# A two-layer graph-attention kernel: the next group's first products moved ahead of the last product, x2 made on VectorE, and three output tiles started from x2 in PSUM

## The reference, cut to what matters

```python
h = jnp.maximum(_layernorm(x), 0.0)
x = x + L0(h, adj)      # 12 heads of 32
h = jnp.maximum(_layernorm(x), 0.0)
x = x + L1(h, adj)      # 6 heads of 64

# L0
v = einsum('bnd,ade->bane', h, W); th = tanh(v)
attn = leaky(th @ w_src + (th @ w_dst)^T); attn = where(~adj, -999, attn); attn = softmax(attn)
feat = elu(attn @ v + b); gate = sigmoid(h @ H_w.T + H_b)
return gate * feat + (1 - gate) * h
# L1
q, k, v = h @ Wq + bq, h @ Wk + bk, h @ Wv + bv
return softmax(q @ k^T / 8 + mask) @ v @ Wf + bf
```

## Time and profile before

| | |
|---|---|
| median of 3 runs | 1011.37 us (1010.96 to 1014.32) |
| the profiled execution | 1006.25 us |
| its span | 1004.5 us |
| granted PE clock, mean of the span | 0.979 |
| PE busy | 926.7 us (92%) |
| PE weight loads busy | 817.8 us (81%) |
| DVE busy | 786.5 us (78%) |
| ACT busy | 641.2 us (64%) |
| POOL busy | 278.5 us (28%) |

### The profile page before, as it was taken

How to read it: one execution, slowest core, us unless ns; L and a number is a source line. 1 busy time by engine, 2 the same in 40 slices (tenths; PEclk the granted TensorE clock), 3 DMA queues, 4 the chain that set the end, 5 groups by cost and what they waited for, 6 DMA issues and landing times.

```text
span 1004.5 us, 24765 instructions
## 1 busy us (share of the span) xinstructions
PE 926.7 (92%) x9851; PEld 817.8 (81%) x9851; DVE 786.5 (78%) x1473; ACT 641.2 (64%) x1309; POOL 278.5 (28%) x337
## 2 busy tenths in 40 slices
PE   6599999999999999999999999999999999999595
PEld 5386888988888898888889888888988888898475
DVE  5877777879777787977778797777879777886804
ACT  5647658484865858486585848658584865857242
POOL 2224050331506033150603315060331506032210
PEclk9799999999999999999999999999999999999887
DMA  8303252231526223152522415252241525221102
GB/s 221 66 3 32 34 97 34 71 42 18 97 33 97 33 69 44 19 96 34 97 33 68 45 20 96 33 97 33 69 45 18 96 34 97 33 59 19 20 32 64
DMA packets 185077, 56.41 MB, mean 56 GB/s; under 512 B 166402, under 2 KB 184964, under 8 KB 184964
## 3 DMA queue, kind: packets, MB, share of 16 engines
q1 hardware_dynamic: 184964, 54.83, 31.2%
HBM read 17.07 MB, written 12.58 MB: 30 GB/s over the span
## 4 chain that ended last, share of the span: by engine, by line
PE 71%; DVE 22%; issue 2%; ACT 1%; SPq 1%; DMA 1%; POOL 0%; ACTq 0%; DVEq 0%; POOLq 0%
PE ps L694 12%; PE ps L696 12%; PE ps L695 12%; PE ps L761 8%; PE ps L765 7%; PE ps L762 7%; PE ps L680 5%; DVE p L1072 4%; DVE mx L1070 3%; DVE p L1044 3%; DVE x L1032 3%; PE ps L774 3%; DVE rs L1040 3%; PE ps L897 3%; PE ps L840 1%
## 5 line engine op out<-in xcount | busy, mean ns | idle before, releaser
L439 POOL TENSOR_TENSOR x_in<-x_in,ee 128x384 f32<-128x384 f32 x64 | 68.5, 1070 | 563.9 <-DVE ee L1057 563.9
L426 POOL TENSOR_TENSOR x_in<-x_in,bf_row 128x384 f32<-128x384 f32 x64 | 84.0, 1342 | 50.6 <-ACT p L459 50.6
L1070 DVE TENSOR_REDUCE mx<-ps 128x6 f32<-128x384 f32 x64 | 35.2, 550 | 75.8 <-PE ps L840 75.8
L1085 DVE COPY_PREDICATED_SCALAR z<-not_adj,masked 128x768 f32 x64 | 69.9, 1092 | 29.4 <-ACT z L550 29.4
L955 DVE TENSOR_TENSOR hT1l<-ps,hT1h 128x384 fp32r<-128x384 f32 x128 | 62.5, 549 | 26.0 <-ACT hT1h L464 26.0
L680 PE MATMUL ps<-ident,p 128*128 128x128 f32 x384 | 54.6, 287 | 26.9 <-DVE p L1044 15.5
L680 PEld LDWEIGHTS ps<-ident,p 128*128 128x128 f32 x384 | 44.6, 146 | 32.6 <-issue 18.3
L513 ACT ACTIVATE ps<-hb_all 128x384 f32<-128x384 f32 x56 | 27.6, 493 | 66.9 <-DVE x_in L1097 66.9
L531 ACT ACTIVATE QT<-ps,bq_col 128x512 f32<-128x512 f32 x48 | 33.0, 688 | 58.4 <-PE ps L765 58.4
L694 PE MATMUL ps<-Wf_hi,hT1h 128*128 128x384 f32 x192 | 67.6, 352 | 1.2 <-DVE x L1032 0.6
L432 POOL TENSOR_TENSOR x_in<-x_in,h 128x384 f32<-128x384 f32 x64 | 64.2, 1035 | 14.4 <-DVE Wf_lo L985 14.4
(11 more groups left out here) (134 smaller groups left out, 2815.7 us busy)
## 6 DMA issues: line engine op xcount, KB each, us to landing
x_in<-in_x_dram SPq DMA_DIRECT2D x16, 768.0 KB, 5.0
V<-v_tok SPq DMA_DIRECT2D x64, 192.0 KB, 5.8
V<-v_tok SPq DMA_DIRECT2D x128, 96.0 KB, 2.4
out_dram<-x_in SPq DMA_DIRECT2D x16, 768.0 KB, 3.5
x<-in_L_gnn_H_w_dram SPq DMA_DIRECT2D x1, 576.0 KB, 6.1
QT<-in_L_gnn_W_dram SPq DMA_DIRECT2D x3, 192.0 KB, 6.9
thT<-in_L_gnn_Wq_dram SPq DMA_DIRECT2D x1, 576.0 KB, 5.5
z<-in_L_gnn_Wk_dram SPq DMA_DIRECT2D x1, 576.0 KB, 6.5
```

What stands on the lines that cost most here:

```text
L426: pool.tensor_tensor(x_in[:, j % 3, t], x_in[:, j % 3, t], bf_row[:], ALU.add).then_inc(x2_biased, 1)
L439: pool.tensor_tensor(x_in[:, i % 3, t], x_in[:, i % 3, t], ee[:, t], ALU.subtract).then_inc(x2_made, 1)
L1070: dve.tensor_reduce(mx1[:, q], bank.rearrange("p (h m) -> p h m", m=N), AX_X, ALU.max).then_inc(max1_made, 1)
L1085: dve.copy_predicated(zu, not_adj[:, tiles].unsqueeze(2).broadcast_to((P, 2, PAIRS0, N)), masked0[:].unsqueeze(2).unsqueeze(3).broadcast_t ...
```

## The change

Five things are moved or replaced.

1. PE: the values of the next group (`first(t)`, formerly the head of the next body) stand in this body behind `attend0`: one tile ahead of the layer-1 turns, three ahead of `attend1`. The turn of `th`, the gate and `wsd` stand behind `Wf`. The turns of `h` stand all four ahead of `scores`. The first `blocks` stands ahead of `Wq`.
2. DVE makes x2 with a fourth instruction in `close` and takes its statistics there; POOL's subtraction is gone. The gate's "times 0.5 plus 0.5" on ACT is gone too: DVE adds 1 and multiplies by -0.5 instead.
3. ACT copies x2 (with bias) of tiles 1 to 3 into the banks of `Wf` ahead of the product (`put_x2`), the product adds onto it, and ACT copies the sum out (`copy_out`). DVE's `add_out` is left for tile 0.
4. The copies of the turned `th` go from DVE to ACT (`copy_thT`); the fourth turn of `th` and `wsd` share a bank.
5. RING, the waits and the order of DVE and ACT follow from these. An entry `spare` fills the ring up to 64.

```diff
         RING = (
-            jobs("th_made", 0, th_made, 4)
-            + jobs("gate_tanh", 0, gate_tanh, 4)
-            + jobs("thT_copied", 0, thT_copied, 4)
-            + jobs("h1_low", 1, h1_low, 4)
...
+            + jobs("values1_made", 1, values1_made, 4)
+            + jobs("h0_low", NEXT, h0_low, 4)
             + jobs("scores1_shifted", 1, scores1_shifted, 4)
             + jobs("probs0T_copied", 0, probs0T_copied, 6)
+            + jobs("attn0_made", 0, attn0_made, 4)
+            + jobs("th_made", NEXT, th_made, 4)[0:1]
             + jobs("probs1T_copied", 1, probs1T_copied, 3)
+            + jobs("th_made", NEXT, th_made, 4)[1:4]
             + jobs("attn1_low", 1, attn1_low, 4)
             + jobs("out_made", 1, out_made, 4)
+            + jobs("thT_copied", NEXT, thT_copied, 4)[0:3]
+            + jobs("srcdst_copied", NEXT, srcdst_copied, 1)
+            + jobs("gate_tanh", NEXT, gate_tanh, 4)
         )
...
+                def put_x2(t):
+                    if x2_by_act(i, t):
+                        act.wait_ge(x2_biased, TILES * j + t + 1)
+                        act.wait_ge(*last_reader(i, job("out_made", t)))
+                        act.activation(ps[:, job("out_made", t) % BANKS, 0:D], x_in[:, j % 3, t], ACT.Copy).then_inc(x2_put, 1)
+
+                def copy_out(t):
+                    if x2_by_act(i, t):
+                        act.wait_ge(final_full, TILES * j + t + 1)
+                        act.wait_ge(out_made, TILES * j + t)
+                        act.activation(x_in[:, j % 3, t], ps[:, job("out_made", t) % BANKS, 0:D], ACT.Copy).then_inc(out_made, 1)
...
-                attend0(0)
-                attend0(1)
-                attend0(2)
-                if real(i + 1):
-                    turn_h0(i, i + 1, 1 - par, range(0, 2))
+                for t in range(TILES):
+                    attend0(t)
+                first(0)
                 if real(j):
                     turn_probs("probs1T_copied", probs1_divided, pair_of, probs1_turned, p1_tile, PAIRS1, j, 3)
-                attend0(3)
+                first(1)
+                first(2)
+                first(3)
                 if real(j):
                     attend1(0)
                     attend1(1)
...
+                        if x2_by_act(i, t):
+                            pe.wait_ge(x2_put, (TILES - 1) * j + t)
...
+                turn_th()
+                gate_of(0)
+                gate_of(1)
+                srcdst()
+                gate_of(2)
+                gate_of(3)
...
                         dve.wait_ge(elu_made, n)
+                        dve.scalar_tensor_tensor(x1[:, t], h0[:, par, t], 1.0, ee[:, t], ALU.add, ALU.subtract).then_inc(h_less_elu, 1)
+                        dve.wait_ge(h_less_elu, n)
+                        dve.wait_ge(gate_tanh, n)
+                        dve.scalar_tensor_tensor(ee[:, t], gate[:, t], 1.0, x1[:, t], ALU.add, ALU.mult).then_inc(gated, 1)
+                        dve.wait_ge(gated, n)
                         dve.wait_ge(x_plus_h, n)
...
+                        dve.scalar_tensor_tensor(x_in[:, i % 3, t], ee[:, t], -0.5, x_in[:, i % 3, t], ALU.mult, ALU.add).then_inc(x2_made, 1)
+                        dve.wait_ge(x2_made, n)
                         row_stats(1, x_in[:, i % 3, t], t, i)
...
+                if real(i) and real(i + 1):
+                    h0_lows(i + 1, range(TILES))
                 shift1(0)
                 shift1(1)
+                divide1(0)
+                divide1(1)
+                divide0(0)
+                divide0(1)
+                divide0(2)
+                divide0(3)
+                close(0)
+                values0(i + 1, 0)
+                values0(i + 1, 1)
+                close(1)
+                if real(j):
+                    for t in range(TILES):
+                        dve.wait_ge(attn1_high, TILES * j + t + 1)
+                        low_tile(hT1l, hT1h, "attn1_low", t).then_inc(attn1_low, 1)
```

More of the change, by code:

```diff
@@ L197, in two_layer_gnn @@
         bias_put = sem("bias_put")
+        x2_put = sem("x2_put")
         bv_spread = sem("bv_spread")
@@ L273, in hw_bank, with th_bank @@
         def hw_bank(c):
-            taken = [job("th_made", t) % BANKS for t in range(TILES - 1)] + [job("h0_low", k) % BANKS for k in range(TILES)]
-            return [b for b in range(BANKS) if b not in taken][c - C]
+            return (job("srcdst_copied", 0), job("gate_tanh", 0), job("th_made", 2))[c] % BANKS
+        def th_bank(t):
+            return (job("thT_copied", t) if t < 3 else job("srcdst_copied", 0)) % BANKS
         def last_reader(i, at):
@@ L619, in body @@
                 exp0(0)
-                if real(i + 1):
-                    normalise0(i + 1, 1 - par)
-                if real(i):
-                    for t in range(TILES):
-                        act.wait_ge(gate_tanh, TILES * i + t + 1)
-                        act.activation(gate[:, t], gate[:, t], ACT.Identity, scale=0.5, bias=half[:]).then_inc(gate_made, 1)
+                copy_q(1)
+                copy_q(2)
                 exp0(1)
                 copy_k(0)
+                if real(i) and real(i + 1):
+                    normalise0(i + 1, 1 - par)
+                exp0(2)
                 copy_k(1)
-                exp0(2)
                 copy_k(2)
+                exp0(3)
+                for t in range(TILES):
+                    copy_values1(t)
                 for q in range(4):
                     put_mask(q)
-                copy_values1(0)
-                exp0(3)
-                copy_values1(1)
-                copy_values1(2)
-                copy_values1(3)
+                if real(i) and real(i + 1):
+                    h0_parts(i + 1, range(TILES))
                 if real(i):
@@ L724, in body, with first @@
                 j = i - 1
-                if real(i):
-                    for t in range(TILES):
+                def first(t):
+                    if real(i + 1):
                         toks = slice(t * P, (t + 1) * P)
-                        pe.wait_ge(h0_low, TILES * i + t + 1)
+                        pe.wait_ge(h0_low, TILES * (i + 1) + t + 1)
                         take(i, job("th_made", t))
-                        if not real(j) and t == TILES - 1:
+                        if not real(i) and t == 2:
                             pe.wait_ge(small_ready, 3)
@@ L748, in body, with turn_th, srcdst @@
                             pe.matmul(dst, ones_rows[:], hb_rows[:], start=False, stop=True).then_inc(gate_full, 1)
-                if real(i):
-                    turn_tokens("thT_copied", th_made, th_turned, lambda t, c: th[:, t, c * P:(c + 1) * P], i, i)
-                if real(j):
-                    turn_tokens("h1_low", h1_made, xn1_turned, lambda t, c: p1_tile(t)[:, c * P:(c + 1) * P], i, j)
+                def turn_th():
+                    if real(i + 1):
+                        for t in range(TILES):
+                            take(i, job("thT_copied", t) if t < 3 else job("srcdst_copied", 0))
+                            pe.wait_ge(th_made, TILES * (i + 1) + t + 1)
+                            for c in range(C):
+                                mm = turn(ps[:, th_bank(t), c * P:(c + 1) * P], th[:, t, c * P:(c + 1) * P])
+                            mm.then_inc(th_turned, 1)
+                def srcdst():
+                    if real(i + 1):
+                        if not real(i):
+                            pe.wait_ge(wsd_made, 2 * 4 * C)
+                        pe.wait_ge(thT_copied, TILES * (i + 2))
+                        for c in range(C):
+                            for t in range(TILES):
+                                mm = pe.matmul(ps[SD * t:SD * t + SD, th_bank(3), D:D + P], wsd[:, c],
+                                               thT[:, c, t * P:(t + 1) * P], start=(c == 0), stop=(c == C - 1))
+                        mm.then_inc(srcdst_full, 1)
                 def project(o, full, name, w):
@@ L818, in body @@
                     values1(3)
+                if real(i) and real(i + 1):
+                    turn_h0(i, i + 1, 1 - par, range(TILES))
                 def masks():
@@ L1016, in values0 @@
                         .then_inc(values0_made, 1)
-            for t in range(TILES):
-                values0(0, t)
-                late_lows(t)
-            source_dest_consts()
             def body(i, par):
```

313 lines of the change are left out of this document (141 added, 172 removed).

## The result

The changed kernel takes **1059.35 us** (median of 4 runs, 1058.31 to 1060.69), against 1011.43 (1010.96 to 1014.32) for the kernel before on the same chip: a ratio of 1.0468, 95% interval 1.0445 to 1.0491. That is slower by 47.9 us.

A forecast was written before the change was run, and what follows sets the result against it. PE was taken as the bound, but not alone: DVE sets the pace behind the layer-1 scores. Bodies +47, head +0.5 and tail -1.5 gave +46 us on 1011.4, so 1057 us, range 1040 to 1071.

The forecast's parts named there:

- Leg 3: End of Wv to the first Wf matmul, where DVE works almost without waiting after its long wait: 23.2 us.
- PE's waits in leg 3: Between end of Wv and first Wf matmul, PE waits 4.0 us in pieces: 23.2 less its own 19.2.
- Leg 2: First Wq matmul to the end of Wv: 20.4 us, 21.23 before less 0.83 for one blocks moved out.
- Leg 4: First Wf matmul to the end of the gate: Wf, gate, turn of th and wsd on PE, 14.76 us.
- Leg 1: End of the gate to the first Wq matmul, set by ACT: stays 3.68 us, 1.45 of it a new wait.
- Body 62.0: One full body as the sum of four legs, against 58.63 us: +3.4 us each, +47 us for 14.
- Head: Up to the first Wq of body 1: values, th and gate in another order behind the same weights, +0.5 us.
- Tail: Body 15 onward: PE loses about what it lost before; Leg 1 and one blocks less give -1.5 us.
- DVE blocked in `softmax0`: POOL's x2 + bias additions block two softmax0 instructions, 2.7 us on DVE; with four blocked, 1093 us. Chance 0.05.
- PE's clock: New waits lower the clock to 0.9 in the legs PE sets: +4 us a body, 1113 us. Chance 0.04.
- Faster: DVE's stretch in Leg 3 shorter than counted: body 58.0, 1002 us, or 982 with ACT's Leg 1 chain hidden. Chance 0.08.
- no change: Leg 3 comes out between 19.6 and 20.1 us, leaving the time as before. Chance 0.04.

The follow-up runs named there:

- the last kernel: Changed kernel with h turned early, masks spread, close late, bias product early, and DVE/ACT order in the head restored; third tanh ahead of normalise1: 1002.04 us, ratio 0.9943.
- the nine other traces: Profiles of nine separate edits of the changed kernel (order, padding, x2, sums, head), 1041.17 to 1074.85 us; last group's stretch 48.1 to 48.6 us at clock 0.85.

## Why the prediction was right

1057 us were forecast, 1059.35 measured. The body is right and for the reasons given; the head is not, and that the total came within 2.4 us all the same is partly luck (see the sum). By its steps:

- *Leg 3, 23.2 us.* Measured 23.13, with DVE's wait of 7.5 (some 7 forecast), `close` 2.84 (2.85) and the fourth instruction 0.59 to the next start (0.6 taken, bounds 0.5 and 0.73). The instruction beside which POOL used to run takes 558 ns in the mean now (L1096) against 732 (L1054), the undisturbed time that was assumed. That DVE sets it is shown by the added microsecond (+1.02) and the removed x2 (-0.84).
- *PE's waits in leg 3, 4.0 us.* Measured 3.8, at the places named, and 0.16 for the masks besides.
- *Leg 2, 20.4.* Measured 20.21.
- *Leg 4, 14.76.* Measured 14.96 (14.88 to 14.97 in the fourteen bodies); adding to DVE there changes nothing.
- *Leg 1, 3.68 with 1.45 of wait.* Measured 3.53. The wait in front of Wq is 0.54, and none stands in front of `blocks`, where part was expected; the rest, 0.7, lies inside the turn of `p`, whose twelve rows span 2.16 us ahead of the body shown, against 1.47, so 1.2 in all. Moving one tanh took 1.0 us off, so ACT sets this leg, as forecast.
- *Body 62.0, +47 us for 14.* Measured 61.81; 14 x (61.81 - 58.64) = +44.4.
- *Head, +0.5 us.* **This term was mis-sized: +8.4 measured** (90.11 against 81.74). I held that the head was the same work behind the same weights, and followed the weights alone. The runs showed that three things came late with the order on DVE and ACT: the low parts of the weights behind all four `values0`, `norm0` of group 1 behind two `softmax0`, the bias product behind a turn that waits for `h`. Putting them back gave 5.5 us, the bias product with POOL's x + h alone 1.3. The remaining 2.9 were not taken apart.
- *Tail, -1.5 us.* **Missed too: +0.8 measured.** Body 15, from its first Wq to that of the last group, takes 1012.10 - 955.47 = 56.63 us against 959.34 - 902.73 = 56.61 before, so what the leg without `wsd` and the moved `blocks` should have given didn't come. PE waited there before once, for ACT's normalised input:

```profile
PE ps L680 <- ACT p L459: 9.9, 1, 9.9
```
  Now both `close` of body 15 stand ahead of the low parts for `Wf`, no values fill PE, and it waits

```profile
PE ps L725 <- DVE hT1l L1003: 4.2, 1, 4.2
PE ps L711 <- ACT p L459: 3.6, 1, 3.6
PE ps L940 <- DVE x L1075: 2.3, 1, 2.3
```
  10.1 us in three pieces: the waits moved and did not shrink. In the last kernel the first is 0.2, and that for `p` 7.1. The 0.8 us lie behind the last group's first Wq (45.9 us against 45.1) and were not taken apart; at the clock of the nine other traces this stretch would have been 2.2 to 2.7 us longer still.
- *Sum.* 44.4 + 8.4 + 0.8 = 53.6 us of span (1058.0 - 1004.5 = 53.5), against +46 forecast: the span was forecast at 1050.5 and came out 7.5 us longer. The median came so near because the profiled execution of before lay 5 us under its median and I added these 5 us, while that of the changed kernel lies at its own. That this hid most of the miss in head and tail is luck.
- *The rivals.* DVE blocked in `softmax0`: the four x2 + bias additions took 1009 ns in the mean instead of 1342, were over (524.6 us) before the first subtraction of `softmax0` (525.49), and leg 2 is 20.21, so no. It is POOL's x + h that now lies beside one: the fourth subtraction of `softmax0` takes 1.45 us in the body shown instead of 0.96, half a microsecond out of DVE's wait of 7.5. PE's clock: 1.00 in the bodies. Faster, or no change: leg 3 under 20.1 didn't come without a change of order; with it, at 17.97, the kernel is level with the one before, and the last kernel (body 58.24, 1002.04 us) is about what the first of these rivals gave for a leg 3 that PE alone sets (58.0 and 1002).

## What to carry to other kernels

An engine with a quarter of its time free can still set the pace: find the place at which its program makes it wait, and count everything between that wait and what the bound engine needs next. Two instructions placed once inside and once outside such a stretch show which side is free. Work that has an alternative place is priced by where it stands, not by its length alone (one `close` of 2.84 us costs at most 1.85 in leg 3, and a microsecond behind `Wf` nothing); and what is moved off one path is late on the next (here `close` ahead of the scale of `normalise1`), so each move wants its own trace. The head is a schedule of its own and has to be walked instruction by instruction like a body.
